# Quantised convolution and attention-like layer over 16 images: the second layer's TensorE work in two visits a quarter instead of four

## The reference, cut to what matters

```python
v = dac(gn(x)); fv = v + 0.1 * v ** 3                 # layer 0, input
outs = [conv3x3(fv, g_pos[i] - g_neg[i]) for i in range(3)]
x = x + (adc(outs[2]) + 4*adc(outs[0]) + 2*adc(outs[1])) * output_factor + bias

z = gn(x)                                             # layer 1
q, k, v = Wq @ z, Wk @ z, Wv @ z                      # 64 x 128 each, per pixel
ek = exp(k)
num, den = exp(B) @ (ek * v), exp(B) @ ek             # 64 x 64
x = x + Wm @ (q * (num / den))                        # 128 x 64
```

## Time and profile before

| what | us |
|---|---|
| median of three runs (1570.87 to 1574.5) | 1571.08 |
| profiled execution | 1572.13 |
| its span, first to last instruction | 1570.1 |
| TensorE busy in the span | 1455.7 (93%) |
| VectorE busy | 1394.0 (89%) |
| ScalarE busy | 1158.4 (74%) |
| GpSimd busy | 504.8 (32%) |

### The profile page before, as it was taken

One profiled execution on the slowest core, in us unless ns is written; L12 is line 12 of the kernel. 1 busy time (PEld: TensorE's weight loads), 2 busy tenths in 40 slices (PEclk: granted clock), 3 DMA queues, 4 the chain that ended last, 5 costly groups with the idle time before them and its releaser, 6 DMA issues.

```text
span 1570.1 us, 22714 instructions
## 1 busy us (share of the span) xinstructions
PE 1455.7 (93%) x7792; PEld 622.6 (40%) x7792; DVE 1394.0 (89%) x2172; ACT 1158.4 (74%) x1505; POOL 504.8 (32%) x506
## 2 busy tenths in 40 slices
PE   1699999999999999999999999999999999999864
PEld 1354434444443444444344433434443444434322
DVE  6869898999989899998989998898999989898646
ACT  4547778787878788787877887787788868776444
POOL 3111333333333333332332423234242423434212
PEclk9799999999999999999999999999999999999988
DMA  5011012313232131323113141321314132111231
GB/s 202 1 54 40 15 28 54 108 28 107 54 94 53 43 108 28 108 55 107 49 38 103 31 115 46 108 54 35 101 33 115 41 108 54 42 40 41 67 81 54
DMA packets 29173, 103.80 MB, mean 66 GB/s; under 512 B 4032, under 2 KB 4224, under 8 KB 29056
## 3 DMA queue, kind: packets, MB, share of 16 engines
q1 hardware_dynamic: 20416, 70.86, 12.3%
q0 software_dynamic: 8640, 31.46, 10.6%
HBM read 37.29 MB, written 33.55 MB: 45 GB/s over the span
## 4 chain that ended last, share of the span: by engine, by line
PE 74%; DVE 18%; issue 4%; ACT 2%; POOL 1%; DMA 1%; DVEq 0%; SPq 0%; POOLq 0%; ACTq 0%
PE A L483 13%; PE A L485 12%; PE A L484 12%; PE L L543 7%; PE B L483 7%; PE B L484 7%; PE B L485 7%; PE L L587 4%; PE L L574 3%; DVE uall L1127 1%; DVE duo L1045 1%; DVE A L1097 1%; DVE duo L1094 1%; DVE uall L1100 1%; DVE q L1017 1%
## 5 line engine op out<-in xcount | busy, mean ns | idle before, releaser
L483 PE MATMUL A<-T,WH 128*128 128x504 f16 (+1 forms) x1152 | 439.6, 382 | 1.0 <-ACT uall L763 1.0
L484 PE MATMUL A<-T,WH 128*128 128x504 f16 (+1 forms) x1152 | 438.1, 380 | 0.0
L485 PE MATMUL A<-T,WL 128*128 128x504 f16 (+1 forms) x1152 | 438.0, 380 | 0.0
L1364 POOL TENSOR_TENSOR T<-t,T 128x512 f16<-128x512 f32 x192 | 244.5, 1298 | 406.8 <-ACT T L696 406.8
L739 ACT ACTIVATE junk<-xr,shift 128x1024 f16<-128x1024 f32 x248 | 284.7, 1148 | 12.0 <-DVE xr L1130 5.2
L1338 POOL TENSOR_TENSOR zl<-z,zh 128x512 f16<-128x512 f32 x120 | 150.8, 1276 | 397.3 <-ACT zh L796 396.3
L483 PE MATMUL B<-T,WH 128*128 128x504 f16 (+1 forms) x576 | 221.7, 385 | 25.5 <-POOL T L1364 16.3
L485 PE MATMUL B<-T,WL 128*128 128x504 f16 (+1 forms) x576 | 220.6, 383 | 0.9 <-issue 0.9
L484 PE MATMUL B<-T,WH 128*128 128x504 f16 (+1 forms) x576 | 220.9, 384 | 0.0
L483 PEld LDWEIGHTS A<-T,WH 128*128 128x128 f16 x1152 | 115.2, 100 | 195.3 <-issue 82.7
L485 PEld LDWEIGHTS A<-T,WL 128*128 128x128 f16 x1152 | 112.7, 98 | 136.4 <-issue 0.3
(11 more groups left out here) (163 smaller groups left out, 2462.1 us busy)
## 6 DMA issues: line engine op xcount, KB each, us to landing
xr<-in_x_dram SPq DMA_DIRECT2D x64, 512.0 KB, 5.9
out_dram<-xr SPq DMA_DIRECT2D x64, 512.0 KB, 2.7
xr<-shared POOLq DMA_DIRECT2D x60, 512.0 KB, 4.6
xr<-in_L_conv_g_pos_dram SPq DMA_DIRECT2D x3, 576.0 KB, 9.5
xr<-in_L_conv_g_neg_dram SPq DMA_DIRECT2D x3, 576.0 KB, 11.3
xr<-in_L_conv_Wm_dram SPq DMA_DIRECT2D x2, 32.0 KB, 9.7
xr<-in_L_conv_Wq_dram SPq DMA_DIRECT2D x1, 32.0 KB, 11.4
xr<-in_L_conv_Wk_dram SPq DMA_DIRECT2D x1, 32.0 KB, 11.3
```

The source lines that it names most:

```text
L483: nc.tensor.matmul(to, wh, th, start=fresh and y == 1, stop=False, skip_group_check=True)
L484: nc.tensor.matmul(to, wh, tl, start=False, stop=False, skip_group_check=True)
L485: done = nc.tensor.matmul(to, wl, th, start=False, stop=y == 2, skip_group_check=True)
L1364: last = nc.gpsimd.tensor_tensor(low, t32[:, pair, :, :, :].rearrange("p t e w -> p (t e w)"), high, ALU.subtract)
```

## The change

Each quarter's work on TensorE is put into two visits. Keys and values of a quarter stand in the same slot as the mix of the quarter before it (`MIX_PE` is `KV_PE` shifted by one), and the queries are computed right ahead of the sums. The queries no longer use `L` but the first bank of `low_pair`; ScalarE copies them from there to SBUF (`copy_queries`, after `guess`), and the mix goes to `low_pair` too, as 64 x 64 tiles of 256 columns. VectorE's ratio and gate become one block of four operations: numerator by queries, denominator by guess, refinement, product. Because `low_pair` is the bank of the convolution's low products, TensorE waits for `m2_copied` before such a visit and for `evicted` or `q_copied` before it uses the bank again (`others_read`, `second_read`).

The order is now given by tables per stage, for the steady state and (`TAIL`) for image 14; most of the other tables are moved by some slots. A value over 35 means the next phase. In phase 16 the two outer products of the last step stand in slot 1.

```diff
-FIRST = 22
-CYCLE = 9
-L2_PE = (1, 3, 6, 7)
-L2_ACT = (1, 3, 6, 8)
-L2_DVE = (2, 5, 6)
-L2_POOL = (6, 8)
-X_STATS = (1, 3, 4, 6)
-X_SPREAD = 7
-X_GROUP = 9
-X_MOMENTS = 9
-COMBINE = (21, 0)
-RESIDUAL = (25, 7)
-X1_STATS = (28, 30, 9, 13)
+KV_PE = (21, 26, 39, 45)
+SUMS_PE = (22, 27, 40, 46)
+KV_ACT = (21, 27, 39, 45)
+MIX_ACT = (27, 39, 45, 57)
+SUMS_ACT = (23, 29, 41, 45)
+Z_ACT = (18, 25, 35, 41)
+KV_DVE = (22, 27, 39, 46)
+SUMS_DVE = (25, 31, 42, 51)
+Z_POOL = (17, 24, 34, 38)
+ADD_POOL = (27, 39, 44, 57)
+TAIL = {"KV_PE": (20, 26, 32, 36), "SUMS_PE": (22, 28, 34, 38), "MIX_PE": (26, 32, 36, 39),
+        "KV_ACT": (20, 26, 32, 36), "SUMS_ACT": (22, 28, 34, 43), "MIX_ACT": (26, 32, 36, 46), "Z_ACT": (18, 23, 29, 35),
+        "KV_DVE": (21, 27, 33, 36), "SUMS_DVE": (23, 29, 35, 44), "Z_POOL": (18, 23, 29, 35), "ADD_POOL": (27, 33, 37, 48)}
+X_STATS = (0, 2, 3, 6)
+X_SPREAD = 9
+X_GROUP = 14
+X_MOMENTS = 15
+COMBINE = (20, 1)
+RESIDUAL = (23, 6)
+X1_STATS = (27, 31, 8, 9)
...
+            def queries():
+                project(low_pair[:, 0, :], 0, 0, crossed=True).then_inc(q_ready, 1)
...
+            def mix(w, out):
+                for part in range(2):
+                    at = slice(part * QUART, (part + 1) * QUART)
+                    for r in range(2):
+                        rows = slice(r * IC, (r + 1) * IC)
+                        for c in range(2):
+                            cols = slice(c * IC, (c + 1) * IC)
+                            last = nc.tensor.matmul(out[r][cols, at], wmf[rows, cols], rec[w][rows, at],
+                                                    start=True, stop=True)
...
+                if mixed:
+                    pe.wait_ge(o_ready, nth(mixed[0], NG, mixed[2]))
+                if values:
+                    keys_values(values[0], values[2], 0)
+                if mixed:
+                    mix(0, (low_pair[:, 0, :], low_pair[:, 1, :]))
+                if summed_up:
+                    queries()
+                    numerator_denominator(summed_up[0], summed_up[2], 0)
...
+                    if slot == 1 and not cur:
+                        outer(p - 1, 1 - m % 2, STEPS - 1, 0)
+                        outer(p - 1, 1 - m % 2, STEPS - 1, 5)
...
+            def copy_queries(image, k):
+                act.wait_ge(q_ready, nth(image, NG, k))
+                nc.scalar.copy(q32, low_pair[:, 0, :]).then_inc(q_copied, 1)
...
             def ratio(image, k, w):
+                dve.wait_ge(q_copied, nth(image, NG, k))
+                nc.vector.tensor_tensor(sums[w][1], sums[w][1], by_half(q32), ALU.mult).then_inc(weighted, 1)
                 dve.wait_ge(guess_ready, nth(image, NG, k))
                 nc.vector.tensor_tensor(sums[w][0], sums[w][0], by_half(rec[w]), ALU.mult).then_inc(rec_ready, 1)
                 dve.wait_ge(rec_ready, nth(image, NG, k))
                 nc.vector.scalar_tensor_tensor(out=by_half(rec[w]), in0=sums[w][0], scalar=2.0, in1=by_half(rec[w]),
                                                op0=ALU.subtract, op1=ALU.mult).then_inc(refined, 1)
                 dve.wait_ge(refined, nth(image, NG, k))
-                nc.vector.tensor_tensor(by_half(rec[w]), sums[w][1], by_half(rec[w]), ALU.mult).then_inc(ratio_ready, 1)
-
-            def gate(image, k, w):
-
-                dve.wait_ge(q_ready, nth(image, NG, k))
-                dve.wait_ge(ratio_ready, nth(image, NG, k))
-                nc.vector.scalar_tensor_tensor(out=rec[w], in0=banks[w][0], scalar=-1.0 / WSCALE, in1=rec[w],
+                dve.wait_ge(weighted, nth(image, NG, k))
+                nc.vector.scalar_tensor_tensor(out=by_half(rec[w]), in0=sums[w][1], scalar=-1.0 / WSCALE,
+                                               in1=by_half(rec[w]), op0=ALU.mult, op1=ALU.mult).then_inc(o_ready, 1)
```

More of the change, by code:

```diff
@@ L117, in conv_layers_kernel @@
         y2 = [shared[:, k * PX:(k + 1) * PX] for k in range(2)]
-        second = [shared[:, 4 * PX + k * HALF:4 * PX + (k + 1) * HALF] for k in range(4)]
+        pieces = [shared[:, 4 * PX + k * HALF:4 * PX + (k + 1) * HALF] for k in range(4)]
         t32 = sb("t32", [P, 3, TILES, 2, W])
@@ L347, in nth, with second @@
             return image * per_image + (m + 1 - back * per_image)
[L349 to L364, removed]
+        STEADY = {"KV_PE": KV_PE, "SUMS_PE": SUMS_PE, "MIX_PE": KV_PE[1:] + (KV_PE[0] + SLOTS,),
+                  "KV_ACT": KV_ACT, "SUMS_ACT": SUMS_ACT, "MIX_ACT": MIX_ACT, "Z_ACT": Z_ACT,
+                  "KV_DVE": KV_DVE, "SUMS_DVE": SUMS_DVE, "Z_POOL": Z_POOL, "ADD_POOL": ADD_POOL}
+        def second(name, p, slot, images):
+            prev2, prev = images[:2]
+            last = B - 1 if isinstance(p, int) and p >= B - 1 else None
+            if prev2:
+                table = TAIL if last and p - 2 == B - 2 else STEADY
+                for k, at in enumerate(table[name]):
+                    if at == slot + SLOTS:
+                        return p - 2, 2, k
+            if prev and (images[2] or not last):
+                table = TAIL if last and p - 1 == B - 2 else STEADY
+                for k, at in enumerate(table[name]):
+                    if at == slot:
+                        return p - 1, 3, k
+            return None
         def phases(eng, phase):
@@ L500, in middle @@
                         pe.wait_ge(m2_copied, nth(p, STEPS, n - 1))
[L502 to L505, removed]
+                    if n:
+                        others_read(p, range(6 * n - 6, 6 * n), images)
+                    elif prev:
+                        earlier = (not (isinstance(p, int) and p <= 2), prev2, True, True)
+                        others_read(p - 1, range(SLOTS - 6, SLOTS), earlier)
                 if j == 1 and (prev or n >= 2):
@@ L576, in numerator_denominator @@
                 last.then_inc(nd_ready, 1)
[L578 to L587, removed]
-                last.then_inc(mix_ready, 1)
@@ new lines, in second_layer @@
+            def second_layer(p, slot, images):
+                n, place = divmod(slot, 6)
+                values, mixed, summed_up = (second(name, p, slot, images) for name in ("KV_PE", "MIX_PE", "SUMS_PE"))
+                if mixed or summed_up:
+                    assert not images[2] or 2 <= place < 5
+                    if images[2]:
+                        pe.wait_ge(m2_copied, nth(p, STEPS, n))
+                        others_read(p, range(6 * n, slot), images)
+                    elif slot == 0:
+                        pe.wait_ge(m2_copied, nth(p - 1, STEPS, STEPS - 1))
+                        others_read(p - 1, range(SLOTS - 6, SLOTS), (True, True, True, False))
+                    else:
+                        others_read(p, range(slot), images)
+                    if X_GROUP == slot and images[3]:
+                        pe.wait_ge(gvar[0], nth(p + 1, 1, 0))
+                    if X1_GROUP == slot and images[1]:
+                        pe.wait_ge(gvar[1], nth(p - 1, 1, 0))
+                if mixed:
[7 more added lines that the diff above has]
+                    numerator_denominator(summed_up[0], summed_up[2], 0)
@@ L1197, in phase @@
                         low_weights(1 + slot // 9, slot % 3)
[L1198 to L1204 removed]
+                    second_layer(p, m, slot, images)
                     if cur and place == 4:
```

177 lines of the change are left out of this document (90 added, 87 removed).

## The result

| | before | after |
|---|---|---|
| median of 7 runs each, taken in turn | 1571.08 us (1569.8 to 1574.5) | 1577.37 us (1575.46 to 1579.12) |
| ratio after / before | | 1.0027 (95% interval 1.0016 to 1.0038) |
| profiled execution, its span | 1572.13, 1570.1 | 1579.12, 1577.4 |
| mean granted clock of TensorE | 0.985 | 0.971 |

The change makes the kernel a little slower (the quotient of the two medians is 1.0040, a little more than the ratio). I had forecast 1560 us and "faster", and had given "slower" 0.13. The time lies within my range of 1537 to 1578 only because that range was wide, and the loss is of the size that the measurement can just tell from no change.

A forecast was written before the change was run, and what follows sets the result against it. TensorE was taken as the bound (89.2 of 90.8 us busy), VectorE close behind. 1572.1 + 4 (steady state) - 15.3 (tail) = 1560.8, brought to the median 1560 us; range 1537 to 1578.

The forecast's parts named there:

- Fewer visits: TensorE's merged second-layer visits: keys, values and mix 2.51 us, queries and sums 1.87, with 0.10 saved per merged boundary.
- The wait at slot 26: TensorE waits 2.5 us (bounds 2.0 to 4.2) for quarter 0's mix, where it waited 1.7 for the ratio.
- VectorE's 0.45 us: VectorE's first residual, ahead of quarter 0's ratio, waits 0.45 us for ScalarE's rounding of step 2.
- The shared bank: Bank B, shared with the convolution's low products: 0 at one-slot places, 0.4 us for late queries at slot 10.
- Rival B: ScalarE holds bank B, TensorE loses 1.5 to 2.5 us more an image: about 1583 us, slower; chance 0.13.
- a period over 92: Sign named for ScalarE holding bank B: period of VectorE's middle mix over 92 us, against 91.0 forecast.
- The period after: Steady state per image: 88.0 + 2.5 + 0.4 = 90.9 us, 91.0 with knife edges, against 90.74 before.
- The tail: Slot 18 of phase 15 to the last convolution matmul: 75.2 to 58.3 us, 15.3 gained after 1.6 given back.
- Rival C: Tail does not shorten, convolution held until quarter 3's ratio, only merges remain: 1572 +- 4 us; chance 0.08.
- The sum: Whole kernel: profiled 1572.1, plus 4 for 14 periods, minus 15.3 for the tail, 1560.8 us; median 1560.
- the head: Phase 0, without a second layer: no change, taken as 0 with bounds -2 and +2 us.
- Rival A: No wait for the mix and the merges pay: steady period 88 to 89.5, about 1535 us; chance 0.17.

The follow-up runs named there:

- Experiment 8: Kernel before with only the mix changed to eight 64x64 matmuls of 256 columns instead of two 64x128 of 512: 1572.58 us, ratio 0.9984.
- experiment 6: experiment 5 with two squares of ScalarE, VectorE's first transform and the high rows behind it two slots later: 1532.12 us, ratio 0.9726.
- experiment 1: Changed kernel with ten added 128x512 matmuls, result never read, ahead of TensorE's wait in slot 26: 1562.26 us, ratio 0.9943.
- experiment 5: experiment 2 with the cast and subtraction of quarter 1 moved ahead of the residual's end: 1570.32 us, ratio 0.998.
- experiment 3: Kernel before with VectorE's cubic one slot earlier, ahead of the ratio, lengthening TensorE's own wait there: 1602.1 us, ratio 1.0196.
- experiment 7: Changed kernel with the last step's outer products back behind image 14's second layer, in slots 4 and 5 of phase 16: 1589.47 us, ratio 1.0088.
- experiment 2: Changed kernel with VectorE taking the ratio of quarter 0 ahead of the first residual, slot 23 instead of 25: 1597.64 us, ratio 1.0157.
- experiment 4: Changed kernel with the last operation of half 0's residual moved behind quarter 0's ratio and a clip done twice more: 1579.6 us, ratio 1.0039.

## Why the prediction was wrong

*Fewer visits: right.* 2.53 and 1.89 us against 2.51 and 1.87; a change of shape costs about 0.1. Experiment 8 shows the mix's new form at no cost, and experiment 6 shows what the visits are worth when nothing waits: 88.85 us with its 0.32 of wait, against 88.0; the rest are delays of up to 0.2 us each, most of them where bank B is shared. My reading that every image from the third to the fourteenth repeats to within 0.1 us was wrong for one, which takes 92.76 in the trace of before (the loss near 950).

*The wait at slot 26: right in place, cause and length.* Keys and values of quarter 0 end (K) where their mix starts, at 742.13, and the waiting visit starts at 757.37, K + 15.2; the wait is 2.36 us where I had 2.5. VectorE's 0.45 us for ScalarE's rounding was 0.33.

*The shared bank: right, and cheaper.* Where TensorE needs the copied queries it loses 0.05 us at a time, and 0.1 in all at slots 9 and 10, where I had put 0.4. Rival B fell: it was to lose 1.5 to 2.5 us there. But the sign that I had given for it, a period over 92, came true all the same, for another reason: a period by itself does not say which wait made it.

*The period after: this step failed, by a term of the sum that was not in it.* I wrote 91.0 and "+0.3 an image". Without the fall of the clock it is 90.80; with it 92.4, over the 1 us at which I had said that the prediction falls. Twelve falls at 1.6 us are 19 of the 20 us that the steady state lost, and experiment 1 gives 14 of them back by filling the idle time. I had the row for it in my hands: the earlier trace rows shows the slow matmuls behind a wait of 3.52, and I charged 1.6 us for it in the tail, but none for a wait that I put at 2.5 in each of 14 images. I had compared 2.5 with the old 1.7 by its length only, though the trace had no example between the harmless 1.61 and the harmful 3.52. The honest bounds for that unknown were 0 and 1.6 an image, 0 to 22 us, and they would have moved the range up and "slower" with it.
The Trainium skill (TensorE: Matmul & The Clock Gate, The HAM clock gate) says that a gate sets TensorE's clock by how busy it has been recently, and that the stretch over which it looks runs free of the program. Twelve falls of 14, 5 of 14 and none at 1.61 agree with that: equal waits end differently. So do the place of the fall, which moves from image to image, and the pairs of experiment 5. How much idle time it takes, and why the longer wait of experiment 3 was followed by a fall in only 5 of the 14 images profiled, stays open; no run here separates what stands around the waits.

*The tail: right in kind, too large a gain.* Between slot 21 and the last convolution matmul TensorE idles for 52.62 - 48.92 = 3.7 us in all, against 3.6. My count, 49.0 us from there without the clock's part, became 52.6: the slow stretch there costs 0.5 in the low half of the keys, 0.9 in the mix and 1.5 in eight convolution matmuls, 2.9 in place of the 1.6 given back. Rival C fell; experiment 7 confirms that the order of the outer products makes most of this gain. The sum also had a slip: the tail was counted from slot 18 of phase 15 but the 14 periods up to slot 21, so the 2.0 us of queries and mix in between, which the last of the 14 periods still contained, were taken off as well. Without it the forecast would have been 1562.

*All together.* My spans differed by -11.3, the measured ones by +7.3: 18.6 us apart. The falls in the steady state are 19.2 of it, the slip 2.0, the tail 2.0 and the serial tail 1.4; the periods without falls (3.2), the head (1.0) and the loss near 950 (2.0) go the other way. That the small terms nearly cancel is luck.

*Rival A* had the right size of the prize and the wrong condition. Experiments 2, 4 and 5 show why the chance was small: behind the wait for the mix stood one for the keys' low half (2.7), behind that the eviction and the weighted values (1.1 and 1.0). All had to move before most of it paid.

## What to carry to other kernels

Price a wait of TensorE twice where TensorE bounds the kernel: by its length, and by the lower clock that may follow; if the trace has no wait of the new length, the second price goes into the bounds. Add up waits that stand close together before you call them short. When a wait lies within one engine's queue, list what else is due just after it before you count its removal as a gain: here the first move made the kernel 1.3% slower than the changed one, with the second it was 0.5% faster, and with all of them 3.0% (the ratios of experiments 2, 5 and 6 over 1.0027).

## What the hardware showed that I had not expected

- Ten useless matmuls (2.33 us) in each of 14 waits made the kernel 15 us faster than with the waits left empty.
- Two waits of 1.15 and 0.96 us, 0.8 apart, brought the lower clock in 7 of 14 images; one of 1.61 never did.
- A GpSimd operation of 2.26 us took 4.53 beside VectorE operations that keep to SBUF, and a VectorE operation of 0.42 us took 1.38 in the same stretch: both sides pay.
- The mix in 64x64 tiles, 16 records of 256 columns, takes 1.02 us, and in 64x128 tiles, 4 records of 512 columns, 1.06: half the tile's width and half the columns, four times the records, the same time.
